# Nine groups of batches in place of eight: two batches in the first and the last, a second copy of the middle stream's sum, and layer 3's condition as a narrow product

## The chip, the cores and the metric

The kernel runs on one core of a Trainium2 chip. The core has five engines with their own instruction queues: TensorE (PE; matmuls and transposes into the eight PSUM banks), VectorE (DVE), ScalarE (ACT), GpSimd (POOL) and SyncE (SP, which here only issues transfers). The metric is the device time of one execution in microseconds, as the median of several runs. Everything is computed in float32.

## The reference

An input x of 32 batches x 128 tokens x 128 features goes through four layers, one after the other:

```
x = L0(x, cond)        # layernorm+modulation, attention (16 heads of 64), gated MLP 128->512->128
x = L1(x, cond)        # rmsnorm+FiLM, attention (1 head of 128), MLP with gelu
x = L2(x, cond)        # layernorm+modulation, attention (16 heads of 8), gated MLP
x = L3(x, cond, mask)  # graph attention over the first 20 tokens as keys, 16 heads of 8, two directions:
#   row_zero = x.sum(-1) == 0 ; q_exp = where(row_zero, 0, cond)
#   self_feat = concat([x, q_exp]) @ W_self.T + b_self
#   aff = where(sum(adj) > 0, q.k/sqrt(8), NEG) + adj @ w_bias + b_bias ; softmax ; @ Wout ; relu ; + x
```

Batches do not touch each other. `cond` is one vector of 128 for each batch, so the part of `self_feat` that comes from it is one vector for each batch, taken or left out for each token by `row_zero`.

## The kernel before

The 32 batches are cut into 8 groups of G = 4, so that 4 x 128 = 512 tokens fill one PSUM bank. Each group goes through four streams, each a list of steps: the front (layer 0's attention; letters A to H), the middle (layer 0's MLP and layer 1; I to P), the back (layer 2; Q to X) and the end (layer 3; a to h). A step is a piece of work such as "the two score products of one pair of heads" (`S`), and every engine has its own part in it. Semaphores tie the parts together.

The order of the work is written out by hand: `ORDERS["all"]` has for each engine a string of 1357 letters, and `weave` gives each letter's stream one step. The strings differ from engine to engine. `order_pairs` lists which step must come before which (a tile that is used again), and `Plan` deals out the PSUM banks along PE's string. Streams of different groups stand between each other, so while group 3 is in its front, group 2 is in its middle and back and group 1 in its end. At the start group A's front has the core to itself. After the last front (H) the strings hold three phases: W, P and f (the back of the seventh group, the middle of the eighth, the end of the sixth); then X and g; then h alone.

What the change and the prediction touch:

- `front`: per pair of heads c (8 of them) the steps `qk`, `v`, `S` (scores), `T` and `T'` (transposed probabilities), `a`, `o`. ACT writes the exponentials (L868), DVE row maxima (L1310) and reciprocals (L1315), POOL the division (L756).
- `back`: `S2`/`T2` units (L1130, L932, L1138), 4 units for each batch, `V2` (L1148), then `o2`, `y2`, `xt`, norm, `up`, `down`. Between its steps, every third one, stand the pieces of the adjacency sums (ACT L927, POOL L786, DVE L1437 and L1438).
- `last`: `adj`, `sum3`, `self3`, `qk3`, then the units `u3` (2 for each batch; PE L1220 scores, DVE L1561 to L1566, POOL L842 and L838, ACT L978, PE L1209 transposes), `a3` (L1201), `y3`.
- layer 3's condition: DVE waits for `sum3` (the row sums of x3, from a product with ones), writes qx = (sum != 0) x cond as a 128 x 512 tile (L1528), and only then PE can do the second product of `self3`, `w3[:, 1, :] x qx` (L1002, `q,w`), onto the first.
- ScalarE's functions lie in tables: a Gelu after an Exp, or an Exp after a Gelu, is preceded by an ACT_TABLE_LOAD. The layer's copies need none of their own.
- `x1` (one tile of 128 x 4 x 128) is what the middle hands to the back; `order_pairs` has the middle of the next group write it only after the back's `y2`.

Of the kernel before, what the change touches and what calls it, by code (L numbers as in the profile page):

```python
# [12 lines left out]
D = 128  # L13
B = 32
G = 4
NG = B // G
# [38 lines left out]
NJ = 2 * G  # L55
# [59 lines left out]
def back_steps():  # L115
    steps = norm_steps(4) + [Step("kq2", 0, ["k2", "q2"], ["k2", "q2"]), Step("v2", 0, ["v2"], ["v2"])]
    for s in range(2 * G + 1):
        for what, lag in (("S2", 0), ("T2", 1), ("T2'", 1), ("E2", 0)):
            w = s - lag
            if not 0 <= w < 2 * G:  # L120
                continue
# [12 lines left out]
def end_steps():  # L134
    steps = [Step("adj", 0, ["adj"], ["adj"]), Step("sum3", 0, ["sum3"], ["sum3"]),
             Step("self3", 0, ["self3"], ["self3"]), Step("qk3", 0, ["q3_0", "q3_1", "k3"], ["q3_0", "q3_1", "k3"])]
    for s in range(NU3 + 5):
        begins, ends = [], []
        if s < 2:
            begins.append(f"vb_{s}")  # L140
            ends.append(f"vb_{s}")
        if s in (S4 + 4, NU3 + 4):
            begins.append(f"a3_{s // S4 - 2}")
            ends.append(f"a3_{s // S4 - 2}")
        if 0 <= s - 4 < NU3:
# [12 lines left out]
FRONTS, MIDS, BACKS, ENDS = "ABCDEFGH", "IJKLMNOP", "QRSTUVWX", "abcdefgh"  # L158
STEPS = {}
for _g in range(NG):  # L160
    STEPS.update({FRONTS[_g]: front_steps(_g + 1 < NG), MIDS[_g]: mid_steps(), BACKS[_g]: back_steps(), ENDS[_g]: end_steps()})
# [7 lines left out]
def edge_slot(i):  # L169

    return i // EDGE_EVERY - 1 if i % EDGE_EVERY == 0 and i >= EDGE_EVERY else None

EDGE_LAST = EDGE_EVERY * (NPIECES + 2)

# [1476 lines left out]
```

## Time and profile before

| | |
|---|---|
| median of 3 runs | 1184.86 us (1183.10 to 1186.69) |
| the profiled execution | 1181.46 us, its span 1179.7 us |
| busy, PE / DVE / ACT / POOL | 1085.0 / 881.7 / 770.1 / 435.8 us |
| mean granted TensorE clock | 0.965 of full speed |
| ACT_TABLE_LOAD | 38, 1283 ns each |

The span runs from the first to the last instruction of the profiled execution; 1.8 us of its own time lie around it. Busy times are unions, so instructions that overlap on one engine count once. A float32 product shows as two PE instructions, so "x256" stands for 128 products. "Idle before" is time in which an engine waited ahead of the instructions of a line, with what released it.

### The profile page before, as it was taken

How to read it: one execution, taken by the hardware profiler on the slowest of the kernel's cores; microseconds unless marked ns; L12 is line 12 of the kernel's file. 1: busy time of each engine (PE TensorE's matmuls, PEld its weight loads, DVE VectorE, ACT ScalarE, POOL GpSimd, SP SyncE). 2: the span in 40 equal slices, each digit the busy share in tenths (PEclk: the TensorE clock that was granted, in tenths of full speed). 3: DMA queues.
4: the chain of work that ended last, by engine and by line, in shares of the span. 5: the costliest groups of instructions: out<-in, count | busy, mean ns of one | idle time of the engine just before them, and what ended most of it. 6: DMA issues, size and time to landing. Idle time of an engine off the chain costs nothing.

```text
span 1179.7 us, 24111 instructions
## 1 busy us (share of the span) xinstructions
PE 1085.0 (92%) x8411; PEld 734.9 (62%) x8411; DVE 881.7 (75%) x2510; ACT 770.1 (65%) x2888; POOL 435.8 (37%) x599
## 2 busy tenths in 40 slices
PE   5898999999999999999999999999989988778675
PEld 4565765776577656676667756766567755546434
DVE  2465767786899687996799788996887678858645
ACT  0655567984788547874789548974678628837712
POOL 1231323431454323542355324541344234515313
PEclk9999999999999989999999999999989999988885
DMA  8000000001000100001000100001000100010000
GB/s 259 2 9 1 11 10 1 10 11 32 1 11 11 32 10 9 2 11 41 1 11 3 39 9 11 2 2 40 1 10 2 41 1 1 2 40 1 1 9 10
DMA packets 21822, 20.98 MB, mean 18 GB/s; under 512 B 1143, under 2 KB 20296, under 8 KB 21448
## 3 DMA queue, kind: packets, MB, share of 16 engines
q1 hardware_dynamic: 18536, 15.26, 4.6%
q10 hardware_dynamic: 3168, 4.19, 1.2%
q8 instruction: 69, 1.13, 0.4%
q14 instruction: 49, 0.40, 0.1%
HBM read 17.35 MB, written 2.10 MB: 16 GB/s over the span
## 4 chain that ended last, share of the span: by engine, by line
PE 68%; DVE 19%; ACT 5%; POOL 4%; issue 3%; DMA 1%; POOLq 0%; DVEq 0%; ACTq 0%
PE bank L1002 11%; PE bank L1021 7%; PE bank L1009 7%; PE bank L1026 5%; PE bank L1047 5%; PE bank L1072 5%; PE bank L1062 5%; PE bank L1056 4%; PE bank L1130 4%; PE bank L1138 3%; PE bank L996 3%; PE bank L1148 2%; PE bank L1220 2%; PE bank L1209 2%; ACT prob_space L932 2%
## 5 line engine op out<-in xcount | busy, mean ns | idle before, releaser
L756 POOL TENSOR_TENSOR fprobs<-fprobs,frinv 128x512 f32<-128x512 f32 x128 | 132.7, 1041 | 249.2 <-DVE frinv L1315 248.3
L932 ACT ACTIVATE prob_space<-bank,negmax 128x128 f32<-128x128 f32 x512 | 181.4, 385 | 34.1 <-DVE negmax L1442 33.9
L868 ACT ACTIVATE fprobs<-bank,fnegmax 128x128 f32<-128x128 f32 x512 | 181.1, 388 | 31.3 <-DVE fnegmax L1310 31.1
L1002 PE MATMUL bank<-fhT,w_qkv 128*128 128x512 f32 x256 | 126.1, 615 | 1.5 <-DVE fv L1324 0.8
L729 POOL TENSOR_TENSOR rstd<-veps,half 128x4 f32<-128x4 f32 x40 | 40.5, 1014 | 208.6 <-DVE veps L1272 173.6
L868 ACT ACTIVATION_READ_ACCUMULATOR fprobs<-bank,fnegmax 128x1 f32 x512 | 116.7, 228 | 0.0
L932 ACT ACTIVATION_READ_ACCUMULATOR prob_space<-bank,negmax 128x1 f32 x512 | 115.7, 226 | 0.0
L1310 DVE TENSOR_REDUCE fnegmax<-bank 128x4 f32<-128x512 f32 x128 | 82.1, 682 | 40.3 <-PE bank L1047 39.8
L1442 DVE TENSOR_REDUCE negmax<-bank 128x4 f32<-128x512 f32 x128 | 82.2, 683 | 22.0 <-PE bank L1130 21.6
L874 ACT ACTIVATE fprobsT<-bank 128x512 f32<-128x512 f32 x128 | 74.5, 605 | 36.5 <-PE bank L1056 36.4
L879 ACT ACTIVATE fk<-bank 128x512 f32<-128x512 f32 x64 | 38.8, 607 | 82.0 <-PE bank L1002 82.0
L1138 PE MATMUL bank<-ident,prob_space 128*128 128x128 f32 x512 | 78.6, 287 | 6.0 <-ACT prob_space L932 5.6
L1056 PE MATMUL bank<-ident,fprobs 128*128 128x128 f32 x512 | 75.8, 279 | 7.6 <-POOL fprobs L756 7.0
L938 ACT ACTIVATE prob_space<-bank 128x512 f32<-128x512 f32 x128 | 76.4, 620 | 8.6 <-PE bank L1138 8.4
L1056 PEld LDWEIGHTS bank<-ident,fprobs 128*128 128x128 f32 x512 | 58.5, 142 | 36.2 <-issue 19.0
L1130 PE MATMUL bank<-km,qk 32*128 32x256 f32 x512 | 75.6, 422 | 3.5 <-POOL km L793 2.2
L1138 PEld LDWEIGHTS bank<-ident,prob_space 128*128 128x128 f32 x512 | 60.6, 147 | 27.3 <-issue 17.6
L1009 PEld LDWEIGHTS bank<-w_qkv,fhT 128*128 128x128 f32 x512 | 65.6, 194 | 19.0 <-issue 16.4
L838 POOL TENSOR_TENSOR p<-p,rinv 128x320 f32<-128x320 f32 x64 | 47.3, 740 | 75.8 <-DVE rinv L1548 75.8
L1047 PE MATMUL bank<-fk,fq 64*128 64x128 f32 x1024 | 74.4, 284 | 0.6 <-issue 0.2
L786 POOL TENSOR_TENSOR adjw<-adjf,labels 80x176 f32<-80x176 f32 (+1 forms) x96 | 53.6, 559 | 54.7 <-ACT adjf L927 54.7
L1047 PEld LDWEIGHTS bank<-fk,fq 64*128 64x128 f32 x1024 | 62.3, 187 | 17.7 <-issue 14.6
(193 smaller groups left out, 2503.6 us busy)
## 6 DMA issues: line engine op xcount, KB each, us to landing
adj<-in_mask_BxSxSx_ik SPq DMA_DIRECT2D x8, 440.0 KB
adj<-in_mask_BxSxSx_ik SPq DMA_DIRECT2D x32, 110.0 KB
x_norm<-in_x SPq DMA_DIRECT2D x8, 256.0 KB, 2.9
x_res<-in_x SPq DMA_DIRECT2D x8, 256.0 KB, 2.8
out<-x_out SPq DMA_DIRECT2D x8, 256.0 KB, 2.3
w_qkv<-in_L_cond_W_qkv ACTq DMA_DIRECT2D x1, 1536.0 KB, 6.9
prob_space<-in_w_mod SPq DMA_DIRECT2D x1, 1024.0 KB
w_up<-in_w_up ACTq DMA_DIRECT2D x1, 768.0 KB, 13.2
```

What stands on the lines that cost most here:

```text
L756: pool.tensor_tensor(p, p, wide(frinv[:, u, :], D), ALU.mult).then_inc(fnormed.sem, 1)
L868: ins = act.activation(fprobs[:, u % NP, b, :], P.bank(("S", u))[:, tok(b)], ACT.Exp, bias=fnegmax[:, u, b:b + 1], accum_out=frsum[:, u, b ...
L932: ins = act.activation(probs[:, u % NP, i, :], P.bank(("A", u))[:, tok(i)], ACT.Exp, bias=negmax[:, u, i:i + 1], accum_out=rsum[:, u, i:i ...
L1002: ins = pe.matmul(P.bank(result)[:, :], w, a, start=(i == 0), stop=(i == len(terms) - 1))
L1009: ins = pe.matmul(P.bank(result)[:, tok(b)], a[:, tok(b)], w, start=(i == 0), stop=(i == len(terms) - 1))
L1021: pe.matmul(P.bank(result)[:, :], w_up[:, l, tok(c)], part.hT[:, :], start=True, stop=True).then_inc(P.full_sem(result), 1)
L1047: ins = pe.matmul(P.bank(("S", 2 * c + r))[:, tok(b)], fq[rows, c % 2, tok(b)], fk[rows, c % 2, tok(b)], start=True, stop=True)
L1056: ins = pe.transpose(P.bank(("T", u))[:, tok(b)], fprobs[:, u % NP, b, :], ident[:, :])
L1130: ins = pe.matmul(P.bank(("A", u))[:, tok(2 * n, 2)], qk[strip(u), 0, tok(b)], flat(km[strip(u), b % 2, 2 * n:2 * n + 2, :]), start=True, ...
L1138: ins = pe.transpose(P.bank(("T", u))[:, tok(i)], probs[:, u % NP, i, :], ident[:, :])
L1310: dve.tensor_reduce(fnegmax[:, u, :], P.bank(("S", u))[:, :].rearrange("p (b k) -> p b k", b=G), AX.X, ALU.max, negate=True).then_inc(fmax ...
L1442: dve.tensor_reduce(negmax[:, u, :], P.bank(("A", u))[:, :].rearrange("p (i k) -> p i k", i=HS), AX.X, ALU.max, negate=True).then_inc(max2 ...
```

## The change

Groups now have sizes 2, 4, 4, 4, 4, 4, 4, 4, 2: nine groups, with letters A to I (front), J to R (middle), S to a (back) and b to j (end). Every tile is cut to the group's size, so a product that had 512 columns has 256 in the two small groups. The back of a small group has 33 steps in place of 51, its end 14 in place of 18, and the adjacency pieces stand on every second step there (10 pieces in place of 12). `x1` has two copies, used in turn, and the pair that held the middle back is now two groups apart. The four order strings are new, 1483 letters each. In layer 3 a product of `w3[:, 1, :]` with the group's 4 (or 2) columns of cond is done in step `adj`; qx is then (sum != 0) x that vector, and DVE adds it in as it drains `self3`.

```diff
 G = 4
-NG = B // G
+SIZES = (2, 4, 4, 4, 4, 4, 4, 4, 2)
+NG = len(SIZES)
+BASE = [sum(SIZES[:g]) for g in range(NG + 1)]
...
-FRONTS, MIDS, BACKS, ENDS = "ABCDEFGH", "IJKLMNOP", "QRSTUVWX", "abcdefgh"
+FRONTS, MIDS, BACKS, ENDS = "ABCDEFGHI", "JKLMNOPQR", "STUVWXYZa", "bcdefghij"
...
-NPIECES = 12
-PIECES = [(0, e, 20) for e in range(0, G * NK3, 20)] + [(1, e, 16) for e in range(0, D, 16)]
-EDGE_EVERY = 3
+PIECES = [[(0, e, 20) for e in range(0, n * NK3, 20)] + [(1, e, 16) for e in range(0, D, 16)] for n in SIZES]
+EDGE_EVERY = [3 if n == G else 2 for n in SIZES]
...
-            "AAAAAAAAAAAAAAAAAAAAAAAAAAAAAAAAAAAAAAAAAAAAAAAAAAAAAAAAAAAAAAAAAAABBAAAAAAAAAIBIBBBBBIBBBBBBIBBIBBI"
+            "AAAAAAAAAAAAAAAAAAAAAAAAAAAAAAAAAAAAAAAAAAAAAAAAAAAAAAAAAAAAAAAABABBBAAABBABBAAABBBBBABABBABBABBBBBB"
...
-        pairs.append((step_at(b, "y2"), step_at(m2, "down", (1, 1))))
+        if g + 2 < NG:
+            pairs.append((step_at(b, "y2"), step_at(MIDS[g + 2], "down", (1, 1))))
...
-        x1 = sb("x1", [D, G, D])
+        x1 = sb("x1", [D, 2, G, D])
...
             def linear(P, result, terms, after=()):
                 banks_free(P, drained=after, empty=[result])
                 for i, (w, a) in enumerate(terms):
-                    ins = pe.matmul(P.bank(result)[:, :], w, a, start=(i == 0), stop=(i == len(terms) - 1))
+                    ins = pe.matmul(P.result(result), w, a[:, 0:P.t], start=(i == 0), stop=(i == len(terms) - 1))
...
                     if what == "adj":
...
+                        ins = pe.matmul(P.bank("adj")[:, 2 * ne:2 * ne + P.n], w3[:, 1, :], condT[:, 1, P.base:P.base + P.n], start=True, stop=True)
...
                     elif what == "self3":
-                        linear(P, "self3", [(w3[:, 0, :], x3T[:, :]), (w3[:, 1, :], qx)], after=["sum3"])
+                        linear(P, "self3", [(w3[:, 0, :], x3T[:, :])])
...
                     if what == "adj":
-                        dve.tensor_copy(gcond[:, :], condT[:, 1, bass.ds(g * G, G)]).then_inc(chain.sem, 1)
-                        dve.wait_ge(*chain.last(g))
                         dve.wait_ge(*P.full("adj"))
+                        ne = P.n * NK3
+                        dve.tensor_copy(gcond[:, 0:P.n], P.bank("adj")[:, 2 * ne:2 * ne + P.n])
...
                     elif what == "self3":
-                        biased(P, "self3", sT[:, :], ROW["L3_cond_b_self"])
+                        c = ROW["L3_cond_b_self"]
+                        dve.wait_ge(*P.drained("sum3"))
+                        dve.wait_ge(*P.full("self3"))
+                        dve.scalar_tensor_tensor(sT[:, 0:P.t], P.result("self3"), col[:, c:c + 1], qx[:, 0:P.t], ALU.add,
+                                                 ALU.add).then_inc(P.free_sem("self3"), 1)
```

PE's last rows, from the transposed adjacency sums of the last group to the first transposes of its units (L1002 and L1033 are the products of `linear`, L1220 and L1255 the scores of the units, L1209 and L1244 the transposes). Before:

```order
L1170 MATMUL bank<-ident,edge 128x80 x2
L1002 MATMUL bank<-x3T,ones 128x512
L1002 MATMUL bank<-x3T,w 128x512
L1002 MATMUL bank<-q,w 128x512
L1002 MATMUL bank<-sT,w 128x512 x2
L1182 MATMUL bank<-sT,w 128x80 x2
L1192 MATMUL bank<-w,kv 80x256 x2
L1220 MATMUL bank<-kbd,q 128x80 x8
L1192 MATMUL bank<-w,kv 80x256 x2
L1220 MATMUL bank<-kbd,q 128x80 x8
L1209 MATMUL bank<-ident,p 80x128 x4
```

And now:

```order
L1203 MATMUL bank<-ident,edge 128x40 x2
L1205 MATMUL bank<-condT,w 128x2
L1033 MATMUL bank<-x3T,ones 128x256
L1033 MATMUL bank<-x3T,w 128x256
L1033 MATMUL bank<-sT,w 128x256 x2
L1217 MATMUL bank<-sT,w 128x40 x2
L1227 MATMUL bank<-w,kv 80x256 x2
L1255 MATMUL bank<-kbd,q 128x80 x16
L1244 MATMUL bank<-ident,p 80x128 x16
L1236 MATMUL bank<-p3T,vb 32x128 x16
L1027 MATMUL bank<-ident,q 128x128 x2
```

The product with qx (`q,w`) is gone, a product with two columns stands ahead, the widths are halved, and 16 score products and 16 transposes are left where there were 32 of each.

ScalarE at the first MLP of the second group's middle stream (`mhid`), beside the third group's front (`fk`, `fprobs`, `fprobsT`). Before:

```order
L868 ACTIVATE fprobs,frsum<-bank,fnegmax 128x128 x8
L879 ACTIVATE fk<-bank 128x512
L874 ACTIVATE fprobsT<-bank 128x512 x2
L868 ACTIVATE fprobs,frsum<-bank,fnegmax 128x128 x4
L893 ACT_TABLE_LOAD
L893 ACTIVATE mhid<-bank,col 128x512 x4
L898 ACTIVATE qk<-bank,col 128x512
L927 ACTIVATE adjf<-adj 128x220
L868 ACT_TABLE_LOAD
L868 ACTIVATE fprobs,frsum<-bank,fnegmax 128x128 x4
```

And now (line numbers of the changed kernel: L924 Gelu, L899 the front's Exp):

```order
L905 ACTIVATE fprobsT<-bank 128x512
L924 ACT_TABLE_LOAD
L924 ACTIVATE mhid<-bank,col 128x512 x2
L905 ACTIVATE fprobsT<-bank 128x512
L899 ACT_TABLE_LOAD
L899 ACTIVATE fprobs,frsum<-bank,fnegmax 128x128 x4
L924 ACT_TABLE_LOAD
L924 ACTIVATE mhid<-bank,col 128x512 x2
L899 ACT_TABLE_LOAD
L899 ACTIVATE fprobs,frsum<-bank,fnegmax 128x128 x4
```

The four Gelus stood together behind one table load; they now stand as two and two, with exponentials between, and four loads around them. Over the whole program ScalarE's rows have 38 loads before and 58 now. The other counts over the whole program: products with 512 columns and full rows 432 before and 371 now, the same form with 256 columns (the back's scores with 32 rows among them) 256 and 362, DVE instructions 2510 and 2623, POOL's tensor operations 584 and 617.

## Rows read from the trace of the kernel before


**Rows 1.** The page: busy time, share of the span and instructions of TensorE.

```profile
PE 1085.0 (92%) x8411; PEld 734.9 (62%) x8411; DVE 881.7 (75%) x2510; ACT 770.1 (65%) x2888; POOL 435.8 (37%) x599
```

**Rows 2.** Stretches: from:to, length, busy time (instructions) by engine, clock, DMA share, GB/s.

```profile
0.00:22.00 22.00, 10.30 (x47) 9.71 (x47) 5.19 (x28) 1.79 (x3) 5.40 (x16) 1.00 0.93 280
22.00:80.00 58.00, 52.80 (x377) 35.30 (x378) 32.12 (x76) 34.13 (x138) 15.57 (x15) 1.00 0.11 31
120.00:540.00 420.00, 411.69 (x3250) 282.33 (x3251) 332.16 (x963) 305.39 (x1171) 163.31 (x209) 0.99 0.05 13
540.00:960.00 420.00, 407.33 (x3240) 276.36 (x3236) 337.07 (x960) 288.83 (x1086) 161.80 (x219) 0.99 0.05 13
960.00:1050.00 90.00, 74.74 (x608) 49.73 (x608) 70.63 (x211) 58.80 (x207) 36.19 (x55) 1.00 0.05 14
1050.00:1133.00 83.00, 66.42 (x494) 42.78 (x494) 57.20 (x160) 49.30 (x188) 29.85 (x50) 0.81 0.00 1
1133.00:1180.00 47.00, 26.79 (x186) 17.16 (x186) 26.77 (x64) 10.24 (x19) 16.04 (x28) 0.69 0.04 12
```

**Rows 3.** The same view, in two stretches of 12 us in the middle.

```profile
600.00:612.00 12.00, 12.00 (x92) 8.17 (x89) 11.15 (x35) 12.00 (x57) 7.19 (x9) 1.00 0.01 3
612.00:624.00 12.00, 10.87 (x126) 8.46 (x126) 11.86 (x30) 9.34 (x42) 6.27 (x9) 1.00 0.01 1
```

**Rows 4.** Timeline, one pair of heads of group A: start, length, engine, instruction, idle before.

```profile
43.57 1.16 PE L1047 MATMUL bank<-fk,fq 64*128 64x128 f32 x16
...
44.76 1.29 DVE L1310 TENSOR_REDUCE fnegmax<-bank 128x4 f32<-128x512 f32 x2 [2.37 <-PE bank L1047]
...
48.68 1.04 POOL L756 TENSOR_TENSOR fprobs<-fprobs,frinv 128x512 f32<-128x512 f32 x1 [0.36 <-DVE frinv L1315]
...
49.77 0.65 PE L1056 MATMUL bank<-ident,fprobs 128*128 128x128 f32 x4 [0.58 <-POOL fprobs L756]
50.36 1.16 PE L1047 MATMUL bank<-fk,fq 64*128 64x128 f32 x16
```

**Rows 5.** TensorE's groups by form, whole span: busy and mean of one, idle before.

```profile
L1026 PE MATMUL bank<-hid,w_down 128*128 128x512 f32 x64 | 29.0, 596 | 0.0
L1192 PE MATMUL bank<-w,kv 128*80 128x256 f32 x64 | 16.6, 382 | 0.0
L1002 PE MATMUL bank<-q,w 128*128 128x512 f32 x16 | 9.1, 651 | 0.0
L1002 PE MATMUL bank<-x3T,w 128*128 128x512 f32 x16 | 9.0, 645 | 4.0 <-DVE q L1528 4.0
L1182 PE MATMUL bank<-sT,w 128*128 128x80 f32 x32 | 5.0, 282 | 0.0
L1238 PE MATMUL bank<-condT,prob_space 128*128 128x32 f32 x32 | 7.0, 402 | 1.1 <-DVE condT L1584 1.1
```

**Rows 6.** TensorE's timeline over the last two phases, at their joints.

```profile
1060.76 1.26 PE L1130 MATMUL bank<-km,qk 32*128 32x256 f32 x16
...
1109.79 1.08 PE L1148 MATMUL bank<-prob_space,vm 128*32 128x128 f32 x32
...
1133.77 1.12 PE L1002 MATMUL bank<-x3T,ones 128*128 128x512 f32 x2 [0.80 <-DVEq L1498]
1136.68 1.12 PE L1002 MATMUL bank<-x3T,w 128*128 128x512 f32 x2 [1.78 <-DVE q L1528]
...
1151.92 1.08 PE L1209 MATMUL bank<-ident,p 128*80 128x128 f32 x4 [4.75 <-POOL p L838]
...
1170.23 1.08 PE L1209 MATMUL bank<-ident,p 128*80 128x128 f32 x4 [0.74 <-POOL p L838]
```

**Rows 7.** ScalarE's timeline around one table load.

```profile
943.70 1.28 ACT L868 ACT_TABLE_LOAD   x1
945.00 0.37 ACT L868 ACTIVATE fprobs<-bank,fnegmax 128x128 f32<-128x128 f32 x1
```

**Rows 8.** VectorE, by form: a small reciprocal.

```profile
L1315 DVE RECIPROCAL frinv<-frsum 128x4 f32<-128x4 f32 x128 | 21.1, 167 | 12.6 <-ACT fprobs L868 12.4
```

More of the change, by code:

```diff
@@ L112, in mid_steps, with back_steps @@
             + mlp_steps(1))
[L115 removed]
+def back_steps(size):
     steps = norm_steps(4) + [Step("kq2", 0, ["k2", "q2"], ["k2", "q2"]), Step("v2", 0, ["v2"], ["v2"])]
[L117 removed]
+    for s in range(2 * size + 1):
         for what, lag in (("S2", 0), ("T2", 1), ("T2'", 1), ("E2", 0)):
             w = s - lag
[L120 removed]
+            if not 0 <= w < 2 * size:
                 continue
@@ L522, in build @@
         adj1 = sb("adj1", [G * NK3, D * L3], I32)
-        PW = max(n for _, _, n in PIECES) * L3
+        PW = max(n for some in PIECES for _, _, n in some) * L3
         adjf = sb("adjf", [D, 2, PW])
@@ L578, in build, with batches, halves, units2 @@
         x_stored = sem("x_stored")
+        def batches(n):
+            return n
+        def halves(n):
+            return n // 2
+        def units2(n):
+            return S4 * n
+        def units3(n):
+            return S4 * n // 2
+        def pieces(n):
+            return n + D // 16
+        def end_links(n):
+            return END_LINKS + units3(n)
         fmod_ready = count("fmod_ready", 1)
@@ L800, in back @@
                         head_keys(0)
-                    elif what == "S2" and k % 2 == 0 and k // 2 + 1 < G:
+                    elif what == "S2" and k % 2 == 0 and k // 2 + 1 < P.n:
                         head_keys(k // 2 + 1)
@@ L1025, in down @@
                 for c in (2 * i, 2 * i + 1):
-                    ins = pe.matmul(P.bank(f"g{l}")[:, :], w_down[:, l, c, :], part.hid[:, c, :], start=(c == 0), stop=(c == FF - 1))
+                    ins = pe.matmul(P.result(f"g{l}"), w_down[:, l, c, :], part.hid[:, c, 0:P.t], start=(c == 0), stop=(c == FF - 1))
                 if i == 1:
@@ L1243, in prologue @@
                 pe.wait_ge(*fz_ready.nth(0, 0))
-                for b in range(G):
+                for b in range(SIZES[0]):
                     ins = pe.transpose(ps[4][:, tok(b)], fz[:, b, :], ident[:, :])
@@ L1258, in statistics @@
             def statistics(chain, g, i, src, k):
-                for b in range(G):
+                n = SIZES[g]
+                for b in range(n):
                     ins = dve.bn_stats(stats[:, i, b, :], src[:, b, :])
@@ L1263, in statistics @@
                 dve.memset(held[:, 0:1], 0.0)
-                for b in range(G):
+                for b in range(n):
                     ins = dve.bn_aggr(mv[:, i, b, :], stats[:, i, b, :])
```

473 lines of the change are left out of this document (241 added, 232 removed).

## The prediction, made before the changed kernel was run

> **What bounds the kernel now.** I read the busy times first, then the stretches, then TensorE's timeline at the start and the end. TensorE is busy 1085.0 us of 1179.7 [rows 1]; the reader is to see where the other 95 us lie [rows 2]. Up to 22 us there is setup, TensorE idle for 12. Group A's front alone (22 to 80) leaves it idle for 5. From 120 to 960 us it is busy 819 of 840 us: the middle is TensorE's, with VectorE at 669 (80%) and ScalarE at 594 (71%) beside it. From 960 us, when no front is left, it is idle for 52 of 220 us: 15, 17 and 20 in the three phases. The clock there falls to 0.81 and 0.69 of full speed. Full speed is 2.4 GHz, the lower level 1.2, so a share f = 2 x (1 - clock) of the time is at half speed and f/2 of the busy time is extra: 0.19 x 66.4 + 0.31 x 26.8 = 21 us. So the ending holds some 73 us that are idle or slow; that is the place where a change of the group sizes can pay, since work taken out of it goes into a middle that runs TensorE at 97.5%.
>
> The sum is made against the profiled execution (1181.5 us); the median of the runs is 3.4 us above it, and the differences are added to the median, 1184.9. About 0.3% (3.5 us) is what a measurement of this kernel can tell from no change.
>
> **The start: -1 us.** With two batches, two of the four modulations ahead of the first product go, some 0.7 us. In the front alone one pair of heads takes 6.8 us from scores to scores (43.57 to 50.36), of which 6.2 are a chain: scores, row maxima, eight exponentials, division, second transposes at 49.77 [rows 4]. With half the batches the exponentials, maxima and division about halve, so the chain is some 3.6 us and the pair 4.0, while TensorE has half of 6.8, 3.4, to do. Six such pairs leave it idle for some 4 us, where the stretch 22 to 80 left 5 [rows 2]. Bounds: -4 (the chain is covered) and +3 (it is 1.2 us longer in half the pairs). I take -1 for the whole start.
>
> **TensorE's work: +1 us.** 53 products with 512 columns become 106 with 256. A 512-column instruction costs 29.0/64 = 0.453 us, a 256-column one 16.6/64 = 0.26 [rows 5], two instructions each: 106 x 0.52 - 53 x 0.906 = +7. The product with qx goes: 9.1 us busy. The nine narrow products come, 18 instructions. No row has 4 columns; the nearest are 80 columns at 5.0/32 = 0.156 and 32 columns at 7.0/32 = 0.22. I take 0.156, +2.8; bounds 0 and 4. Together +1.
>
> **The wait ahead of self3: -2 us.** TensorE waited 4.0 us in all for qx, 1.8 of them in the last group [rows 5, 6]. Now both products issue without it, and VectorE adds qx while it drains the second. The other 2.2 us lie where TensorE is short of other work; the last 1.8 are counted with the ending. VectorE's drain now waits for its own qx, which stood there before as well. Bounds: -2.2 and 0.
>
> **The ending: -11 us.** Half of one middle, of one back and of one end leave it.
> - First phase (Z, R, h in place of W, P, f). VectorE is the fuller engine against its means, 70.6 of 90 us. Two phases' difference gives a middle as 70.6 - 57.2 = 13.4 us of VectorE [rows 2]; half of it less, 63.9 at the same 78% share, is 82 us: -8.
> - Second phase (a and i in place of X and g). By the chain: 16 units took 49 us (1060.76 to 1109.79) [rows 6], 8 take 24.5; the 10.8 us ahead of them become 8, the 24 behind them 17, since products, drains and statistics halve: 49.5 us. By VectorE: an end alone is 26.8, so the back is 57.2 - 26.8 = 30.4 [rows 2], half of it 15.2 and 1 for fixed costs, with the end 43; at a 78% share 55 us, at this phase's 69% 62. I take 56: -27.
> - Third phase (j in place of h). The last transposes follow each other every (1170.23 - 1151.92)/7 = 2.6 us [rows 6]; four units fewer are 10.5. The wait of 1.78 for qx goes, and the halved products and drains before the units give some 2: -14, 33 us.
>
> The ending would be 171 us in place of 220. Half of one stream of each kind is about a quarter of its TensorE work (it holds one middle, two backs, three ends): 168 us busy less 21 for the slow clock is 147, a quarter of it 37, and at the middle's 97.5% that costs 38 us there. -49 + 38 = -11. Bounds: +2 with 62 us in the second phase, 85 in the first and 36 in the third, and -20 with 49, 80 and 32.
>
> **What grows beside TensorE: +5 us.** ScalarE has 20 more table loads (58 against 38 rows). One takes 1.28 us, and from its start at 943.70 to the next exponential at 945.00 pass 1.30 [rows 7]: 26 us. VectorE has 113 more instructions of the small kind, at 0.17 us [rows 8] some 19 us. Such time lies beside TensorE's wherever the engine has room. ScalarE is full in few stretches of the middle, as from 600 to 612 us, VectorE in somewhat more, as from 612 to 624, where TensorE is down to 10.87 [rows 3]. Of the 70 stretches of 12 us from 120 to 960 us, 8 have ScalarE over 11.5 us busy and 13 VectorE. 26 x 8/70 + 19 x 13/70 = 3.0 + 3.5; a part of VectorE's lies in the ending, which I have counted, so 5. Bounds 0 and 26.
>
> On the loads the Trainium skill speaks against the change (page "ScalarE: Activation LUTs", section "What ACT_TABLE_LOAD costs"): a load of 1283 ns is followed by a drain of about 1380 ns, 2.66 us a switch; by it the 20 loads would be 53 us of ScalarE, and the term above 3.1 us more. This trace agrees with the first figure and shows no drain: the exponential begins 0.02 us behind the load.
>
> **The new order of the middle: -3 us.** The second `x1` frees the middle stream from the back of the group ahead, but I find no wait of that kind in the trace; what it changes is the order. Each front now overlaps the next by 18 to 55 steps of TensorE's string, where only the first three did before, by up to 17, so the crowded and the empty zones of VectorE lie less against each other. Idle time of 21 us and about 1% of slow clock (some 8 us) are all that could be won, -29. Nothing says how much; the same amount could be lost, as the strings are fixed and a late engine holds all behind it. I take -3, bounds -25 and +20.
>
> Sum: -1 + 1 - 2 - 11 + 5 - 3 = -11, 1174 us.
>
> **The rivals.**
> - A, the ending gives it back (no change). Its phases are chains between engines, and VectorE's share stays at 69 to 78% with half-full tiles, whose fixed costs stay. Then the phases are 85, 62 and 36 us, 37 saved and 38 paid: the sum loses its -11 and is 1185, in the forecast's other terms unchanged. For it: the second phase is 55 to 62 by VectorE, and a small back finds a full-size end beside it. Against: the halved count of units is exact.
> - B, the middle too becomes denser. The overlapped fronts fill the holes of VectorE's crowded zones; 15 us of the 29 come: 1160. For it: TensorE is idle just where VectorE is full [rows 3]. Against: no wait in the trace is one that the change takes away.
> - C, slower: the table loads. They stand between the exponentials of a front and those of a back, and PE's transposes, POOL's divisions and the bank of the scores wait behind them. If all loads are on that path, 26 us come in place of 3.0, 1174 + 23 = 1197. It decides from some 17 us on (13 of the 20 loads exposed), 1174 + 14 = 1188. For it: in the second group's middle two loads have become four within one MLP, and each pushes a front's unit. Against: TensorE is idle for 21 us in the whole middle, whatever it waits for, beside 38 loads, and ScalarE is idle 29% of it [rows 2].
> - D, by the skill's price, with the drain behind each load and all exposed: 20 x 1.36 = 27 above C, 1224. The trace speaks against it.
> - E, the change doesn't shorten the ending since the last group waits for its adjacency transfer (issued nine steps before the small back starts, where the pieces now begin at its second step). The size of the transfer is halved; worth up to 5 us, and inside A.
>
> **How the numbers follow.** Forecast 1174 (1167 to 1182): 0.42. A, with E, 1180 to 1190: 0.19. B, 1150 to 1167: 0.18. C, 1188 to 1205: 0.20. D: 0.01. Faster means under 1181.3: 0.38 of the forecast, all of B and 0.06 of A, 0.62. Within 0.3% (up to 1188.4) lie 0.04 of the forecast and 0.12 of A, 0.16. Slower are 0.01 of A, C and D, 0.22. The range 1154 to 1196 leaves out the low end of B, the upper half of C and D, some 0.15; the likeliest case alone is 1167 to 1182.
>
> **What would show it.** In the changed profile: from the last front's end to the end of the span some 171 us, with 82, 56 and 33; the last phase without a wait of `x3T,w` for VectorE's q; the middle with TensorE busy at 97% or more; 58 loads of 1283 ns with TensorE's idle time that ends with an exponential under 20 us; the row of narrow products under 4 us. The forecast is wrong if the small phases keep the length of the large ones (A), if TensorE's idle time ahead of the transposes that wait for L932's and L868's successors grows by 10 us and more (C), or if the middle's idle share falls under 1.5% (B).

## The result, and the profile after

The changed kernel takes 1166.4 us (median of 4 runs, 1163.1 to 1167.6) against 1184.0 (1182.3 to 1186.7) for the kernel before on the same chip: ratio 0.985, 95% interval 0.982 to 0.988, or 17.6 us less. The forecast was 11 less, 1174 (1154 to 1196). The profiled executions have spans of 1179.7 and 1164.6 us, a difference of 15.1; the one of the kernel before is 2.5 us under its kernel's median.

The busy times of the changed kernel, which answer to [rows 1]:

```profile
PE 1080.4 (93%) x8525; PEld 752.7 (65%) x8525; DVE 894.3 (77%) x2623; ACT 807.3 (69%) x2956; POOL 446.9 (38%) x632
```

TensorE works 4.6 us less and idles 10.5 us less. The stretches say where (columns as in [rows 2]; the last three are the phases of the ending, cut where TensorE turns (transposes) the edges' sums, which is the first thing an end stream does):

```profile
0.00:22.00 22.00, 10.62 (x47) 9.87 (x48) 4.89 (x22) 1.79 (x3) 5.04 (x16) 1.00 0.93 292
22.00:80.00 58.00, 54.32 (x385) 38.05 (x384) 34.70 (x111) 36.08 (x147) 17.29 (x24) 1.00 0.05 14
80.00:120.00 40.00, 39.85 (x301) 28.42 (x300) 26.97 (x74) 26.70 (x101) 12.55 (x14) 1.00 0.05 15
120.00:987.03 867.03, 842.95 (x6768) 583.74 (x6767) 699.77 (x2061) 649.42 (x2383) 344.97 (x467) 0.99 0.05 14
987.03:1074.77 87.74, 75.00 (x578) 52.21 (x576) 67.28 (x193) 55.80 (x203) 34.02 (x56) 0.88 0.02 4
1074.77:1135.75 60.98, 44.93 (x353) 32.01 (x352) 45.93 (x126) 32.76 (x111) 25.35 (x44) 0.83 0.03 8
1135.75:1164.60 28.85, 12.73 (x103) 8.43 (x102) 14.72 (x38) 4.75 (x10) 7.69 (x14) 0.65 0.05 14
```

Of the kernel before, the stretches with the same joints that [rows 2] doesn't have:

```profile
80.00:120.00 40.00, 34.93 (x219) 21.48 (x218) 20.53 (x55) 21.62 (x79) 7.61 (x8) 0.96 0.00 1
951.27:1047.64 96.37, 81.12 (x654) 52.96 (x653) 76.33 (x238) 59.97 (x209) 37.19 (x56) 1.00 0.05 13
1047.64:1132.67 85.03, 66.43 (x495) 42.78 (x494) 58.68 (x164) 49.23 (x187) 29.85 (x50) 0.82 0.00 1
1132.67:1179.70 47.03, 27.09 (x190) 17.31 (x188) 27.10 (x65) 10.31 (x19) 16.04 (x28) 0.70 0.04 12
```

- **Start.** TensorE's idle time up to 120 us falls from 22.0 us (12 + 5 in [rows 2], 5.1 behind them) to 15.2: -6.8.
- **Middle.** It grows from 831 us (120 to 951.3, TensorE busy 812.3) to 867 (842.9): idle 18.9 and 24.1 us, +5.2. TensorE is busy at 97.2%.
- **Ending.** 96.4 + 85.0 + 47.0 = 228.4 us become 87.7 + 61.0 + 28.9 = 177.6: 50.8 less, with 42.0 us less of TensorE's work in it, so idle time falls by 8.9.
- **Together:** -6.8 + 5.2 - 8.9 - 4.6 (work) = -15.1.

The 4.6 us less of work are the clock's. Cut into stretches of 2 us, the sum of (1 - clock) x busy time is 33.9 us before and 27.7 now; at full speed TensorE would be busy 1051.1 and 1052.7 us, 1.6 more (an estimate from these stretches).

Of the middle's idle time, what ends with an exponential of ScalarE has grown from 0.9 to 7.3 us, most of it here (engine, tile, line and what it waited for: us in all, times, longest us; before from 120 to 951 us, now from 120 to 987):

```profile
PE bank L1138 <- ACT prob_space L932: 0.7, 2, 0.4
PE bank L1170 <- ACT prob_space L963: 4.0, 7, 1.5
```

The last phase on TensorE's timeline (start, length, instruction, and in brackets the idle time before it with its releaser), for [rows 6]:

```profile
1135.75 0.32 PE L1203 MATMUL bank<-ident,edge 40*128 40x40 f32 x2
1136.00 0.38 PE L1205 MATMUL bank<-condT,w 128*128 128x2 f32 x2
1136.68 0.70 PE L1033 MATMUL bank<-x3T,ones 128*128 128x256 f32 x2 [0.30 <-DVEq L1534]
1137.21 0.59 PE L1033 MATMUL bank<-x3T,w 128*128 128x256 f32 x2
1139.16 1.13 PE L1033 MATMUL bank<-sT,w 128*128 128x256 f32 x4 [1.35 <-DVE sT L1570]
...
1150.01 1.08 PE L1244 MATMUL bank<-ident,p 128*80 128x128 f32 x4 [5.94 <-POOL p L869]
...
1156.09 1.07 PE L1244 MATMUL bank<-ident,p 128*80 128x128 f32 x4 [1.28 <-POOL p L869]
```

`x3T,w` follows the sum's product without a wait. A part of that wait has moved one link on: the next product waits 1.35 us for sT, which VectorE can only make when it has made qx. Over the whole span the waits for sT grow from 0.8 us (in the last group) to 2.9 (in the last two), so of the 4.0 us of waits for qx 1.9 are saved. The groups by form, for [rows 5] (line, engine, shapes, count, busy us, mean ns, idle before):

```profile
L1033 PE MATMUL bank<-fhT,w_qkv 128*128 128x256 f32 x64 | 18.2, 409 | 0.3 <-DVE fhT L1321 0.3
L1033 PE MATMUL bank<-x3T,w 128*128 128x512 f32 x14 | 7.4, 608 | 0.0
L1205 PE MATMUL bank<-condT,w 128*128 128x4 f32 x14 | 2.4, 245 | 0.0
L1033 PE MATMUL bank<-x3T,w 128*128 128x256 f32 x4 | 1.2, 388 | 0.0
L1205 PE MATMUL bank<-condT,w 128*128 128x2 f32 x4 | 0.8, 262 | 0.0
```

The group of qx and w, 9.1 us before [rows 5], is gone; the narrow products take 3.2 us.

### The profile page after: what moved, and what is told of

It is laid out like the page before. It is cut to its first block, busy times and chain, and to the rows that moved or that the text cites. A ratio compares the mean times of both kernels' runs of the same rounds, so it can differ in the third digit from the quotient of the medians.

```text
span 1164.6 us, 24661 instructions
## 1 busy us (share of the span) xinstructions
PE 1080.4 (93%) x8525; PEld 752.7 (65%) x8525; DVE 894.3 (77%) x2623; ACT 807.3 (69%) x2956; POOL 446.9 (38%) x632
## 4 chain that ended last, share of the span: by engine, by line
PE 64%; DVE 18%; ACT 13%; issue 2%; POOL 2%; DMA 1%; SPq 0%; POOLq 0%; DVEq 0%; ACTq 0%
PE bank L1033 11%; PE bank L1041 7%; PE bank L1053 6%; PE bank L1079 5%; ACT prob_space L963 5%; PE bank L1094 4%; PE bank L1058 4%; PE bank L1104 4%; PE bank L1088 4%; PE bank L1162 3%; PE bank L1170 3%; PE bank L1027 3%; ACT fprobs L899 2%; PE bank L1180 2%; PE bank L1255 2%
## 5 line engine op out<-in xcount | busy, mean ns | idle before, releaser
L786 POOL TENSOR_TENSOR fprobs<-fprobs,frinv 128x512 f32<-128x512 f32 (+1 forms) x144 | 136.1, 950 | 253.3 <-DVE frinv L1351 252.1
L899 ACT ACTIVATE fprobs<-bank,fnegmax 128x128 f32<-128x128 f32 x512 | 181.4, 381 | 54.3 <-DVE fnegmax L1346 53.8
L1033 PE MATMUL bank<-fhT,w_qkv 128*128 128x512 f32 (+1 forms) x288 | 125.5, 559 | 0.3 <-DVE fhT L1321 0.3
L1346 DVE TENSOR_REDUCE fnegmax<-bank 128x4 f32<-128x512 f32 (+1 forms) x144 | 83.9, 624 | 44.8 <-PE bank L1079 43.9
L899 ACT ACTIVATION_READ_ACCUMULATOR fprobs<-bank,fnegmax 128x1 f32 x512 | 111.8, 219 | 0.0
L759 POOL TENSOR_TENSOR rstd<-veps,half 128x4 f32<-128x4 f32 (+1 forms) x45 | 42.4, 943 | 148.8 <-DVE veps L1308 112.6
L905 ACT ACTIVATE fprobsT<-bank 128x512 f32<-128x512 f32 (+1 forms) x144 | 76.5, 557 | 28.8 <-PE bank L1088 28.5
L1170 PE MATMUL bank<-ident,prob_space 128*128 128x128 f32 x512 | 81.5, 293 | 9.9 <-ACT prob_space L963 9.1
L817 POOL TENSOR_TENSOR adjw<-adjf,labels 80x176 f32<-80x176 f32 (+2 forms) x104 | 58.9, 568 | 67.2 <-ACT adjf L958 67.0
L910 ACT ACTIVATE fk<-bank 128x512 f32<-128x512 f32 (+1 forms) x72 | 40.3, 560 | 62.8 <-PE bank L1033 62.7
L1170 PEld LDWEIGHTS bank<-ident,prob_space 128*128 128x128 f32 x512 | 62.1, 150 | 32.1 <-issue 16.0
L1079 PE MATMUL bank<-fk,fq 64*128 64x128 f32 x1024 | 77.4, 288 | 3.5 <-DVE p L1601 1.6
L1079 PEld LDWEIGHTS bank<-fk,fq 64*128 64x128 f32 x1024 | 63.7, 189 | 21.4 <-issue 18.9
```

Source lines behind the costliest of these rows:

```text
L786: pool.tensor_tensor(p, p, wide(frinv[:, u, 0:P.n], D), ALU.mult).then_inc(fnormed.sem, 1)
L899: ins = act.activation(fprobs[:, u % NP, b, :], P.bank(("S", u))[:, tok(b)], ACT.Exp, bias=fnegmax[:, u, b:b + 1], accum_out=frsum[:, u, b ...
L905: act.activation(flat(fprobsT[:, u % NP, 0:P.n, :]), P.result(("T", u)), ACT.Copy).then_inc(P.free_sem(("T", u)), 1)
L1033: ins = pe.matmul(P.result(result), w, a[:, 0:P.t], start=(i == 0), stop=(i == len(terms) - 1))
L1079: ins = pe.matmul(P.bank(("S", 2 * c + r))[:, tok(b)], fq[rows, c % 2, tok(b)], fk[rows, c % 2, tok(b)], start=True, stop=True)
L1170: ins = pe.transpose(P.bank(("T", u))[:, tok(i)], probs[:, u % NP, i, :], ident[:, :])
```

## The experiments

Ratios are to the kernel before, timed on the same chip; a step of 0.0015 in a ratio is 1.8 us. The runs were timed on several chips, so "above the changed kernel" is the difference of two such ratios, times 1184 us. Joints and stretches come from one profiled execution of each kernel. "Joint" is the time at which TensorE turns a group's edges; from group to group it tells where a kernel gains or loses. For the changed kernel the nine joints are 245.5, 372.4, 501.2, 652.2, 772.3, 883.7, 987.0, 1074.8 and 1135.7 us.

### 1. The old form of the condition in the changed kernel

```diff
-linear(P, "self3", [(w3[:, 0, :], x3T[:, :])])
+linear(P, "self3", [(w3[:, 0, :], x3T[:, :]), (w3[:, 1, :], qx)], after=["sum3"])
-ins = pe.matmul(P.bank("adj")[...], w3[:, 1, :], condT[...], ...)       # the narrow product
-dve.scalar_tensor_tensor(sT[...], P.result("self3"), col[...], qx[...], ALU.add, ALU.add)
+biased(P, "self3", sT[:, :], ROW["L3_cond_b_self"])
```

> The changed kernel with layer 3's condition in its old form again: a second product of 512 (or 256) columns per group, taken into the bank of the first, and the copy of the condition by the group. Theory (TensorE's work counts one for one): about 9 us of products come back, 3.2 us of narrow ones go, and the product waits again for VectorE's comparison, some 2 us over nine groups, so +6 to +9 us on the 1166 of the changed kernel, 1172 to 1175. Rival (the products stood where TensorE waited anyway): under 2 us, 1166 to 1168.

Measured: 1182.7 us, ratio 0.9991 (0.9975 to 1.0008). That is 16.8 us above the changed kernel, twice what the theory gave, and no measurable gain on the kernel before: nine groups in the new order are worth -1.1 us (-3.0 to +0.9) without the new form of the condition. Up to the fourth, its joints are even 0.5 to 1.7 us earlier than the changed kernel's; then they are 4.0, 4.4, 7.1, 7.4 and 14.2 us later, and the end is 16.6 later. The first loss stands here on TensorE's timeline:

```profile
652.25 1.02 PE L1033 MATMUL bank<-x3T,ones 128*128 128x512 f32 x2
...
657.06 2.08 PE L1033 MATMUL bank<-x3T,w 128*128 128x512 f32 x2 [2.92 <-DVE q L1563]
```

The same place in the changed kernel:

```profile
652.95 1.02 PE L1033 MATMUL bank<-x3T,ones 128*128 128x512 f32 x2
...
654.69 1.02 PE L1033 MATMUL bank<-x3T,w 128*128 128x512 f32 x2
```

The product starts 4.8 us behind the sum's instead of 1.7, waits 2.92 us and then takes 2.08 us instead of 1.02: the granted clock is down to its lower level behind the wait (0.57 on average from 656 to 660 us). In most groups other work stands between the two products (the second starts 7.6 us behind the first in the first group, 4.2 in the second) and nothing is waited for; the new order puts them close together in three groups, this one and the last two. The waits are 6.3 us in all. The kernel before has waits in three groups too, 4.0 us in all [rows 5], one of them in its last phase.

### 2. The narrow product in the old groups and the old order

This kernel also has the two copies of x1.

```diff
-SIZES = (2, 4, 4, 4, 4, 4, 4, 4, 2)
+SIZES = (4, 4, 4, 4, 4, 4, 4, 4)      # and the strings of the kernel before
```

> The kernel before (eight groups of four batches, its own order of steps on every engine) with the narrow product for the condition and the two copies of the middle stream's sum. Theory: -6 to -9 us on the 1184 of the kernel before, 1175 to 1178, so that about half of the change's 17.6 us is this part alone. Rival: it stood in slack, -2 us or less, and the groups and the order give all of it.

Measured: 1178.4 us, ratio 0.9953 (0.9940 to 0.9965), -5.6 us (-7.1 to -4.1). That is at the lower end of the theory's -6 to -9, and not the rival's value. Up to the fifth joint it had gained more, 9.1 us (813.4 against 822.5). 5.6 of them come between the second and the third joint (130.3 us against 136.0), where no x3T,w wait was. The stretches of the kernel before there (columns as in [rows 2]):

```profile
424.00:432.00 8.00, 7.66 (x30) 3.96 (x28) 7.83 (x21) 4.41 (x19) 3.01 (x4) 1.00 0.01 3
432.00:436.00 4.00, 2.13 (x11) 1.51 (x12) 3.77 (x10) 0.00 (x0) 1.59 (x3) 0.81 0.00 0
436.00:444.00 8.00, 8.00 (x26) 4.78 (x24) 4.91 (x11) 5.08 (x26) 1.72 (x5) 0.50 0.00 0
444.00:448.00 4.00, 4.00 (x18) 2.51 (x18) 1.66 (x5) 2.82 (x4) 2.70 (x7) 0.91 0.01 2
```

With the narrow product:

```profile
424.00:428.00 4.00, 4.00 (x16) 2.03 (x14) 3.90 (x13) 1.56 (x3) 1.72 (x2) 1.00 0.01 2
428.00:432.00 4.00, 1.93 (x16) 1.53 (x16) 3.85 (x9) 0.08 (x1) 2.89 (x4) 1.00 0.00 0
432.00:440.00 8.00, 8.00 (x39) 4.65 (x38) 6.32 (x15) 7.97 (x31) 3.90 (x11) 1.00 0.00 0
```

Both kernels have a hole of 2.1 to 2.2 us ahead of a product of keys (`km,qk`, at 433.9 and 430.2 us). In the kernel before it is followed by half clock: 0.19 x 4 + 0.5 x 8 + 0.09 x 4 = 5.1 us of work not done. With the hole 3.7 us earlier the clock stays at its full level. What decides this the rows don't tell. Later the reverse happens: from the fifth to the seventh joint this kernel takes 232.2 us where the kernel before takes 225.1, with a clock of 0.89 against 1.00 from 960 to 990 us, so 7.0 of the 9.1 us are given back. These are two single executions, which end 3.1 us apart, where the medians are 5.6 apart.

### 3. The wait alone, and the work alone, in the changed kernel

```diff
 # the wait alone
-linear(P, "self3", [(w3[:, 0, :], x3T[:, :])])
+linear(P, "self3", [(w3[:, 0, :], x3T[:, :])], after=["sum3"])
 # the work alone
-linear(P, "self3", [(w3[:, 0, :], x3T[:, :])])
+linear(P, "self3", [(w3[:, 0, :], x3T[:, :]), (w3[:, 0, :], x3T[:, :])])
```

> The changed kernel, whose first product of x3T by w waits again until VectorE has made the comparison from the sum; no work is added. With the old form of the condition as a whole the changed kernel became 16.8 us slower, with 9.7 us of added products, 3.2 us of removed ones, and waits ahead of that product of 2.9, 0.2, 1.8 and 1.4 us. Theory (the order of the changed kernel has the product straight behind the sum in three groups, so the wait is exposed there, and TensorE's granted clock falls behind it): +5 to +9 us. Rival (work is all): +2 us or less.

> The changed kernel with a second product in that place that waits for nothing (x3T by w once more, so the sum is that product twice and the output another): 9.7 us of work are added, no wait. Theory: +7 to +11 us, about one for one. Rival (TensorE has gaps in which a product costs nothing, and the wait is all): +3 us or less.

Measured: 1174.2 us, ratio 0.9925 (0.9897 to 0.9954), and 1174.5 us, ratio 0.9925 (0.9898 to 0.9952). Each is 9.0 us above the changed kernel (some 4.6 either way), at the upper end of the first theory (5 to 9) and in the middle of the second (7 to 11); both rivals fall. Their sum, 18, agrees with the 16.8 of experiment 1 (which is rid of 3.2 us of narrow products). The wait lasts 2.47, 1.65 and 1.26 us in three groups, 5.4 in all. By the times alone it needn't cost more than that (9.0 less 4.6 is 4.4); the joints say where it does. The first, at 654 us, costs about its own length: the clock stays at 1.00 behind it, and the next joint is 2.2 us late where the one ahead was 0.6 us early. The other two stand in the ending. The last joints of the kernel with the wait alone are 1077.5 and 1145.4, and the two stretches behind them answer to the last two of the changed kernel:

```profile
1077.52:1145.37 67.85, 51.97 (x354) 35.33 (x352) 45.91 (x126) 32.74 (x111) 25.07 (x44) 0.72 0.03 8
1145.37:1175.70 30.33, 14.56 (x103) 9.23 (x102) 14.87 (x38) 4.74 (x10) 7.68 (x14) 0.64 0.05 13
```

VectorE and ScalarE have the same work to 0.02 us (45.9, 32.7), the clock is 0.72 instead of 0.83, TensorE's busy time 7.0 us longer and the phase 6.9; its idle time is the same, 15.9 against 16.1 us. So with a wait of 1.65 us more at its head, the phase pays the whole in slow clock. Not all of the 6.9 us need be the wait's: with no such wait the same phase takes 61.0, 63.9 and 62.1 us in experiments 6, 7 and 8, at clocks of 0.83 and 0.79 in the first two. With the wait it takes 67.9 us here and 67.8 in experiment 1. The work alone shows the like: with four more products (3.1 us) by the fifth joint it is 0.8 us late there, and 8.4 at the end, its second-last phase 64.1 us long at a clock of 0.76.

### 4. The size of the groups without the new order

```diff
-SIZES = (4, 4, 4, 4, 4, 4, 4, 4)
+SIZES = (2, 4, 4, 4, 4, 4, 4, 2)      # the strings lose the steps a half group hasn't
```

> The kernel before, with narrow products, its first and last group halved (28 of the 32 batches are computed, four are left out) and its own order of steps, less the steps that a half group hasn't. Read by its stretches, not by its total. Ending from the edges' transposes of the last group but one: 96/85/47 us before and 88/61/29 after the change. Theory (the size of the last group makes the two last phases short): about 90/62/30 here too, in the old order. Rival (it's the order): the last two phases stay above 70 and 35. Start: if the small first group gives the 6.8 us, TensorE idles some 15 us up to 120 us here; if the order does, 20 us or more.

Measured (a single execution, 1059.5 us, of a kernel that leaves out four batches), the start and the three phases:

```profile
0.00:120.00 120.00, 102.94 (x707) 75.22 (x709) 66.73 (x213) 64.11 (x243) 35.42 (x54) 0.99 0.21 65
870.91:966.67 95.76, 79.91 (x592) 55.81 (x591) 68.48 (x210) 56.82 (x206) 34.69 (x56) 0.84 0.03 9
966.67:1029.14 62.47, 44.89 (x353) 31.53 (x351) 45.14 (x128) 31.21 (x108) 25.55 (x44) 0.78 0.00 1
1029.14:1057.40 28.26, 12.59 (x103) 8.37 (x102) 14.50 (x38) 6.29 (x11) 7.70 (x14) 0.69 0.05 14
```

The last two phases, 62.5 and 28.3 us, are the changed kernel's (61.0 and 28.9), and not those of experiment 2, which differs in the size alone (86.3 and 44.8): they come with the size of the group. The first, 95.8, is about as long as before (96.4), at a clock of 0.84 (changed kernel 0.88, before 1.00). But it takes 100.9 us in experiment 2 and 100.7 in the kernel before without Gelu (experiment 6), so what size gives there lies between nothing and 5 us, and how much of the changed kernel's 8.6 comes with the order stays open. TensorE idles 17.1 us up to 120 us, against 22.0 before and 15.2 after the change: the small group alone brings 4.9 of the start's 6.8 us.

### 5. The new start order with groups of four

The first 140 to 151 steps of each engine's string in the changed kernel's relative order of the first two fronts and the first middle.

> The kernel before, with the first 140 to 151 steps of each engine in the relative order that the changed kernel gives to its first two front groups and the first middle group; the groups stay at four batches. What the start saved (6.8 us of TensorE's idle time up to 120 us) is due to the order or to the small group. Theory (order: the second group's steps join earlier, so the hole at 80 to 120 us, 5.1 us, closes): -4 to -6 us, 1178 to 1180. Rival (small group: with four batches the first heads take 6.8 us each and the second group, as long, covers nothing more): 1183 or more.

Measured: 1202.0 us, ratio 1.0153 (1.0130 to 1.0176), 18.1 us slower. The theory falls. The rival's "1183 or more" holds, but its reason (no more cover than before) would give no change, and not 18 us. The idle time up to 120 us falls (22.0 to 17.6), so the order alone takes 4.4 us of it; the two shares, 4.9 and 4.4, are more than the 6.8 of both together. Then the bill comes:

```profile
0.00:120.00 120.00, 102.42 (x727) 71.46 (x728) 62.87 (x168) 61.62 (x250) 33.98 (x44) 1.00 0.23 67
120.00:150.00 30.00, 23.63 (x161) 15.57 (x159) 18.84 (x59) 16.75 (x54) 6.52 (x7) 0.95 0.06 18
150.00:180.00 30.00, 17.61 (x53) 10.48 (x54) 7.79 (x27) 7.15 (x16) 5.57 (x5) 0.65 0.00 0
```

Both fronts are used up early, and the first middle is then alone with its chains, where TensorE's timeline has:

```profile
147.62 1.11 PE L996 MATMUL bank<-ident,mz 128*128 128x128 f32 x4 [5.10 <-DVE mz L1278]
...
170.40 1.11 PE L996 MATMUL bank<-ident,mz 128*128 128x128 f32 x4 [4.58 <-DVE mz L1278]
```

Here idle time that was filled early, by work that had covered a later chain, was not saved. The third front would have had to come earlier too, which this run didn't do; so it shows what the transplant costs, not what the best order for groups of four would be.

### 6. No table loads

Both kernels are run without the Gelu; their hidden layers' values are left as they are.

```diff
-ACT.Gelu
+ACT.Identity
```

> The changed kernel with the identity in place of every Gelu (so the hidden layers' values are left as they are): of the same size and place on ScalarE, but no table has to be changed for it, so the table loads fall from 58 to a few and 55 x 1.3 = 72 us go from ScalarE's busy time. Theory (loads lie beside TensorE): 5 to 15 us less than 1166, 1151 to 1161. Rival (loads exposed): 17 us or more less by the 20 loads more that the change has, so 50 us or more less in all.

> The kernel before with the identity in place of every Gelu: loads fall from 38 to a few, 46 us less on ScalarE. Theory: 4 to 10 us less than 1184. What the change's 20 further loads cost is the difference of the two differences: 1 to 5 us by the theory, 17 to 26 us by the rival.

Measured: 1166.0 us, ratio 0.9856 (0.9824 to 0.9889), and 1185.0 us, ratio 1.0013 (0.9989 to 1.0037). The pages give 737.5 us busy for ScalarE in the first (807.3 with the loads) and 725.4 in the second (770.1). Of the loads, these are left in the changed kernel's version:

```profile
L884 ACT ACT_TABLE_LOAD x1 | 1.3, 1283 | 1.3 <-PEq L1682 1.3
L899 ACT ACT_TABLE_LOAD x1 | 1.3, 1283 | 0.0
```

In the changed kernel itself there are 58, its three largest groups:

```profile
L924 ACT ACT_TABLE_LOAD x28 | 35.9, 1283 | 0.5
L899 ACT ACT_TABLE_LOAD x21 | 26.9, 1283 | 0.4
...
L1009 ACT ACT_TABLE_LOAD x7 | 9.0, 1283 | 0.1
```

Without 56 loads, 72 us of ScalarE, the changed kernel is no faster (0.8 us slower, some 4.9 either way), nor is the kernel before without 36 (1.5 us slower, some 2.8 either way). Both lie outside what the theory gave. The difference of the two, the price of the 20 further loads, is 0.7 us with about 5.6 either way: rival C, which needed 17 us, falls, and the theory's 1 to 5 us can't be told from nothing. TensorE's waits in the middle that end with an exponential, 7.3 us in the changed kernel, are still 6.6 us without the loads, 3.6 of them here (from 120 to 987 us); so their growth comes with the order and not with the loads:

```profile
PE bank L1170 <- ACT prob_space L963: 3.6, 6, 1.5
```

### 7. A single copy of x1

```diff
-x1 = sb("x1", [D, 2, G, D])       ... x1[:, g % 2, :, :]
+x1 = sb("x1", [D, 1, G, D])       ... x1[:, 0, :, :]
```

> The changed kernel with a single copy of the middle stream's sum. Both reader and writer are VectorE's, and on VectorE and TensorE the order of the changed kernel still puts the readers of one group ahead of the writer of the next. Theory: nothing waits, 1166 within 1.5 us. Rival: the second copy is what lets the middle run on, +5 us or more.

Measured: 1168.6 us, ratio 0.9867 (0.9849 to 0.9885), 2.1 us above the changed kernel, some 3.8 either way. By the times alone this is unclear. The joints say more: 244.8 to 1074.2 us, all 0.6 to 0.9 us ahead of the changed kernel's through eight groups, in which a missing copy would have to show; only the last phase but one is longer, 63.9 us against 61.0. The second copy brings nothing that shows.

### 8. An attempt at a faster version

In the changed kernel's middle the clock falls to 0.50 at 824 to 828 us, behind this wait:

```profile
821.20 1.13 PE L1162 MATMUL bank<-km,qk 32*128 32x256 f32 x8 [1.04 <-DVE fhT L1321]
```

```diff
 # VectorE's string alone, at the last front's first turn: X is the back stream, H the front
-...HXXH...
+...HHXX...
```

> The changed kernel, with one step moved on VectorE alone: the scaling of the last front group's first turned tile (fhT) stands ahead of the maxima of a unit of the back stream, behind which it stood; TensorE waited 1.04 us for it at 821 us and the granted clock was 0.50 from 824 to 828 us. Theory (what the clock takes hangs on such holes, 1.6 us within 4 here): without this one the clock stays at 1.00 there, 3 to 5 us less, 1162 to 1164. Rival (the maxima come later, so TensorE waits at the next transposes instead, and the clock falls all the same): within 1.5 us of 1166.4.

Measured: 1166.7 us, ratio 0.9842 (0.9812 to 0.9871), -0.8 us, some 4.6 either way. That is the rival's value; the times alone would leave room for the theory's -3 to -5, and the trace decides. TensorE's timeline of this run:

```profile
820.35 1.13 PE L1162 MATMUL bank<-km,qk 32*128 32x256 f32 x8
822.39 0.61 PE L1244 MATMUL bank<-ident,p 128*80 128x128 f32 x4 [0.91 <-ACT prob_space L963]
```

And two of its stretches:

```profile
824.00:828.00 4.00, 2.28 (x20) 1.91 (x17) 3.06 (x9) 4.00 (x19) 1.66 (x2) 0.70 0.00 0
828.00:832.00 4.00, 4.00 (x26) 3.62 (x26) 1.91 (x5) 3.44 (x14) 2.51 (x4) 0.50 0.01 4
```

The wait for fhT is gone and one for ScalarE's exponentials stands in its place, since the maxima that they need come later; the clock falls a few us later, and the sixth joint is 1.6 us later than the changed kernel's. VectorE is busy for all of the 4 us from 820 us, so here an exchange moved the wait and didn't remove it. No run beat the changed kernel by more than the noise.

## Why the prediction was right in its size and wrong in one step

The sign, the range and the order of size hold; the time is 7.6 us below the forecast, just under the likeliest case's own range (1167 to 1182) and inside rival B's (1150 to 1167), whose mechanism did not happen (below). That the total came near is in part luck. By the two profiled executions the terms miss by -5.8 us (start), -5.6 (TensorE's work, through the clock), +2 (the wait, which lies in the other stretches' idle time), +2.1 (ending) and +3.2 (middle), together -4.1, so they cancel in part.

- **The ending, -11.** Right, and by its mechanism. 50.8 us saved for 49, by phases 8.6, 24.1 and 18.2 for 8, 27 and 14; phases 88, 61 and 29 for 82, 56 and 33 (the joints here lie 9 us ahead of the forecast's cut at 960 us, so the savings compare better); moved work 42 us for 38. Idle time falls by 8.9 us. That size shortens the last two phases is shown (experiment 4, one execution). In the last phase the transposes of the units follow each other every (1156.09 - 1150.01)/3 = 2.0 us, for the 2.6 taken. Rival A, which needed 37 us saved and a last phase of 36, is out. The second phase was judged too short: its share of VectorE is 75% (45.9 of 61.0) for the 78% taken, and it has 45.9 us of it for 43.
- **The start, -1.** Mis-sized: -6.8 us of idle time. The small group alone takes 4.9 of them (experiment 4), the order alone 4.4 (experiment 5). The pair of heads takes 4.03 us (37.95 to 41.98) for the forecast 4.0, and the first front product comes at 21.33 us, but I ended the account at 80 us. The 5.1 us that TensorE idled from 80 to 120, where group A's front runs out and the first middle begins, were not in it. The smaller group ends sooner, the second front is under way by then, and 0.15 us of idle time are left.
- **TensorE's work +1 and the wait -2: the step that failed.** The single sizes are right: qx's products 9.1 us gone, narrow ones 3.2 us for 2.8, an instruction of 256 columns 18.2/64 = 0.28 us for 0.26, and the work as a whole +1.6 us at full clock for +1. Of the wait 1.9 us are saved net, not the 4.0 (2.2 here and 1.8 in the ending). What failed is that this part was priced as if it were the same in both orders, and with the clock left out of its terms. -9.1 + 2.8 - 2.2 - 1.8 = -10.3 us was its value in the sum. Measured, it is -5.6 us in the old order (experiment 2) and -16.8 in the new one (experiment 1), half of it work and half of it the wait (experiment 3). The new order puts the two products close together in three groups; with the old form it exposes the wait there, the last two times in the ending, where the clock was down for much of the phase. In the old order most of what the narrow form had gained went again with a lower clock (experiment 2).
- **Groups and order.** All else in the sum was -11 + 10.3 = -0.7 us: start, ending, 7 us for the split products, the growth beside TensorE, and the new middle. Measured without the new form: -1.1 (-3.0 to +0.9). That agrees, so the part of the change that fills nearly the whole diff brought nothing measurable by itself, and the 17.6 us are the two together: -5.6 and -1.1 alone, -10.9 (some 3.9 either way) that neither has without the other. A part of it is the clock: (1 - mean clock) x span, the median of each kernel's runs, is 48.5 us for the kernel before, 47.0 with the narrow form alone (experiment 2), 41.4 with groups and order alone (experiment 1) and 36.1 with both, of which 3.8 us neither has without the other (an estimate from the runs' mean clocks). Where the other 7 us come from is not shown; the waits alone, 6.3 us in the new order for 4.0 in the old, are too few.
- **What grows beside TensorE, +5.** Perhaps too high on ScalarE. 3 us were for the 20 loads; the experiment gives 0.7, with an uncertainty of 5.6, so 3 isn't excluded either. VectorE's part wasn't tried by itself.
- **The middle's order, -3.** Not told apart from the rest. Idle time there is 24.1 us of 867 (2.8%, before 18.9 of 831, 2.3%), so it did not become denser: rival B's mechanism is out. TensorE's idle time that ends with an exponential is 14.5 us over the whole span, under the 20 of the forecast, but it was 6.3 before; experiment 6 puts the middle's part of that growth down to the order. (The last two fronts overlapped before as well, by 6 steps, which the prediction passes over.)
- **Rivals D and E.** By the Trainium skill (page "ScalarE: Activation LUTs", section "What ACT_TABLE_LOAD costs") 56 loads are 56 x 2.66 = 149 us of ScalarE, an estimate. The busy time fell by 69.8 us without them, 1.25 a load, which is about the load's own 1283 ns; no idle time stands behind the load of [rows 7], where the exponential begins 0.02 us later; and the kernel's time didn't fall measurably. Nothing here shows the drain. E: ScalarE waited 4.9 us for the adjacency transfer in the second-last phase, with no loss that can be told.

What stays open: where most of the 10.9 us comes from, what share of the clock's fall in the ending is due to the order of steps, and why two nearly equal holes at 428 and 432 us are followed by different clocks.

## What to carry to other kernels

A wait costs what it costs in the order at hand: when a change moves steps and removes a dependence, time each alone and both together, since the dependence may be what keeps the new order from paying (-5.6 and -1.1 us apart, -17.6 together). Split the last group where the ending is chains between engines: with half a group the last two phases are 24 and 18 us shorter and the one ahead of them 9, and 42 us of TensorE's work left the ending for elsewhere, so the gain is only the difference, 8.9 us. A function's table loads on an engine that is 69% busy beside a full TensorE (here 72 us of them) brought nothing that could be measured when they were taken out; look for idle time that they end before editing for them.

## What the runs showed of the hardware

- The granted clock can add to the price of a hole. A wait of 1.65 us at the head of a phase came with 0.72 in place of 0.83 over 68 us, and 6.9 us more (experiment 3), of which up to 3 may be chance. In the middle a wait of 2.92 us was followed by 0.57 over 4 us (experiment 1), and one of 2.47 us at the same place by 1.00 (experiment 3); a hole of 2.2 us was followed by 0.50 over 8 us and more, 5.1 us of work, and another of 2.1 us was not (experiment 2).
- Two kernels that differ in one step ran alike to within a microsecond for 600 us and more: up to the fourth joint the kernels of experiments 3, 7 and 8 are within 1.0 us of the changed kernel. The clock falls at the same places too: in stretches of 20 us from 120 us on it is 1.00 up to 820 us in all of them, and then 0.83. So a difference between two profiles can be dated by one landmark per group before any row is compared.
